# Routing stage of a graph layer with experts: layer-norm sums taken from the quotient, squared deviations on the scalar engine

## The reference

```python
x = x + gnn(xn) + mix(xn)
h = (x - mean(x)) / sqrt(var(x) + 1e-5)
logits = h @ gate_w + gate_b
idx = argmax(softmax(logits));  prb = its probability
pos = cumsum(one_hot(idx)) * one_hot(idx) - 1        # place of the row at its expert
buf[idx, pos] = h                                     # dropped when pos >= C
y = relu(buf @ w1[e] + b1[e]) @ w2[e] + b2[e]
x = x + y[idx, pos] * prb
```

## Time and profile before

| | us |
|---|---|
| time, three runs | median 3505.42 (3503.37 to 3508.54) |
| profiled execution | 3478.89, its span 3477.1 |
| routing stage, from the first instruction to the last scatter's end | 2908.4 to 3008.4 |
| first instruction of `experts` | 3014.1 |
| busy over the span | PE 2543.0, DVE 2333.8, POOL 1813.2, ACT 1147.3 |

### The profile page before, as it was taken

The page is one execution under the profiler, slowest core; times in us unless marked ns, Lnnn a source line. Parts: engine busy times, 40 slices in busy tenths (PEclk is TensorE's granted clock), DMA queues, the critical chain, the costliest instruction groups (busy, mean ns, idle before and its releaser), DMA issues. The chain is left out here.

```text
span 3477.1 us, 46302 instructions
## 1 busy us (share of the span) xinstructions
PE 2543.0 (73%) x11245; PEld 1939.2 (56%) x11245; DVE 2333.8 (67%) x7089; ACT 1147.3 (33%) x4204; POOL 1813.2 (52%) x1892
## 2 busy tenths in 40 slices
PE   8577777777777777794676656566666757599998
PEld 6465555656555556683555544444544536476766
DVE  6788887878787778884555545556666668353535
ACT  5543443434343434341222110122332202334342
POOL 0366666666666666304666666666666663311112
PEclk9789998989888989897787777777787775699999
DMA  6566777777767777314555654643444443412120
GB/s 198 161 189 202 205 206 206 207 203 207 203 202 199 205 205 202 103 57 125 149 156 153 169 161 121 181 112 107 112 113 113 112 115 105 138 49 87 54 90 13
DMA packets 230864, 512.62 MB, mean 147 GB/s; under 512 B 49248, under 2 KB 116043, under 8 KB 230610
## 3 DMA queue, kind: packets, MB, share of 16 engines
q0 software_dynamic: 118128, 361.70, 37.1%
q1 hardware_dynamic: 97958, 134.64, 12.8%
q10 hardware_dynamic: 14524, 13.40, 1.1%
HBM read 463.94 MB, written 49.57 MB: 148 GB/s over the span
## 5 line engine op out<-in xcount | busy, mean ns | idle before, releaser
L1306 POOL DMA_INDIRECT weights<-table,SRC x880 | 840.3, 955 | 599.2 <-issue 234.0
L808 POOL DMA_INDIRECT w_G<-table,SRC x880 | 848.0, 964 | 506.2 <-issue 236.5
L910 PE MATMUL PS<-w_G,w_S 128*128 128x260 f32 x3520 | 936.8, 423 | 120.7 <-DVE ACC L986 100.9
L910 PEld LDWEIGHTS PS<-w_G,w_S 128*128 128x128 f32 x3520 | 715.8, 210 | 256.1 <-issue 127.9
L1485 PE MATMUL PS<-weights 128*128 128x257 f32 x1760 | 592.5, 483 | 56.5 <-issue 28.0
L1680 DVE TENSOR_TENSOR ACC<-ACC,PS 128x257 f32 x464 | 196.3, 423 | 451.8 <-remote 247.1
L1485 PEld LDWEIGHTS PS<-weights 128*128 128x128 f32 x1760 | 396.3, 244 | 143.8 <-issue 64.0
L986 DVE TENSOR_TENSOR ACC<-ACC,PS 128x520 f32 x464 | 320.3, 690 | 201.0 <-remote 120.6
L841 ACT ACTIVATE w_G<-w_G 128x64 f32<-128x64 f32 x1760 | 444.3, 335 | 7.1
L979 DVE TENSOR_TENSOR w_G<-w_G,PS 128x512 f32<-128x512 f32 x660 | 432.3, 682 | 4.7 <-ACT ACC L847 4.2
L1325 ACT ACTIVATE w_PW<-w_Z 128x4 f32<-128x4 f32 x220 | 45.2, 205 | 930.6 <-DVE w_Z L1665 731.2
(11 more groups left out here) (323 smaller groups left out, 3309.6 us busy)
## 6 DMA issues: line engine op xcount, KB each, us to landing
w_DR<-rows SPq DMA_DIRECT2D x146, 384.0 KB
weights<-in_L_ffn_w SPq DMA_DIRECT2D x16, 1024.0 KB, 7.9
w_G<-table,SRC POOLq DMA_INDIRECT x880
weights<-table,SRC POOLq DMA_INDIRECT x880
table<-ACC SPq DMA_DIRECT2D x49, 260.0 KB
xbuf<-XR SPq DMA_DIRECT2D x8, 1040.0 KB
XR<-xbuf SPq DMA_DIRECT2D x7, 1040.0 KB, 5.8
table<-row ACTq DMA_DIRECT2D x49, 129.0 KB, 2.2
```

The costliest lines, as they stand in the source:

```text
L808: pool.indirect_dma_start(G[:, r, b, :], None, table, IndexOn(ap=SRC[:, n * B + b:n * B + b + 1], axis=0)).then_inc(fetched[r], 16)
L910: last = pe.matmul(PS[:, 2 * at + a, 0:W // layer.banks], lhsT, rhs, start=b == slots[0], stop=b == slots[-1])
L1306: pool.indirect_dma_start(G[:, r, b, :], None, table, IndexOn(ap=SRC[:, n * B + b:n * B + b + 1], axis=0)).then_inc(fetched[r], 16)
```

## The change

`quotient` writes the row's sum as well (`accum_out`). `bn_stats` and six of the seven operations of `spread` go; what is left of it, the product of the sum with the gate's column sums, becomes `means(g)` and moves to the head of `choose(g)`. The scalar engine computes the squared deviations: `square(t)` takes `(sum - 256 x)^2` with the sum as its bias and accumulates over the row, two tiles ahead of the copy (`SQUARES = 2`). The root takes that sum with scale and epsilon folded in. `sums` issues plain quotients, no longer one ahead: with AHEAD still 3, the quotients up to b + 2 stand before `choose(g)` and those up to b + 4 before `assign(g)`.

```diff
-AHEAD, LEAD, ROOT = 3, 3, 2
+AHEAD, LEAD, ROOT, SQUARES = 3, 3, 2, 2
             def quotient(t):
-                dve.scalar_tensor_tensor(x1(t), ACC[:, t, 0:D], RD[:, t:t + 1], x1(t), ALU.mult, ALU.add).then_inc(x1_ready, 1)
-
-            def statistics(t):
-                dve.wait_ge(x1_ready, t + 1)
-                return dve.bn_stats(bn[:, t, :], x1(t))
+                dve.scalar_tensor_tensor(x1(t), ACC[:, t, 0:D], RD[:, t:t + 1], x1(t), ALU.mult, ALU.add,
+                                         accum_out=total[:, t:t + 1]).then_inc(x1_ready, 1)
             def sums(a, b):
                 for t in range(a, b):
-                    if t == 0:
-                        quotient(0)
-                    if t + 1 < TILES:
-                        quotient(t + 1)
-                    last = statistics(t)
-                    if t + 1 in AT:
-                        own_.link(last)
-                        spread(AT.index(t + 1) - 1)
-            def spread(g):
+                    quotient(t)
+
+            def means(g):
...
-                own_.link(dve.tensor_tensor(ta[:, s], bn[:, s, 1], bn[:, s, 4], ALU.subtract))
-                own_.link(dve.scalar_tensor_tensor(ta[:, s], ta[:, s], 0.25, ta[:, s], ALU.mult, ALU.mult))
-                own_.link(dve.tensor_tensor(va[:, s], bn[:, s, 2], bn[:, s, 5], ALU.add))
-                own_.link(dve.tensor_scalar(va[:, s], va[:, s], 1.0 / D, EPS, ALU.mult, ALU.add))
-                dve.tensor_tensor(ta[:, s], ta[:, s], va[:, s], ALU.add).then_inc(to_root, 1)
-                own_.link(dve.tensor_tensor(me[:, s], bn[:, s, 1], bn[:, s, 4], ALU.add))
-                own_.link(dve.tensor_tensor(LG[:, s, :], one(me[:, s], 2, EXPERTS), one(gs[:, :], 1, w), ALU.mult))
+                dve.wait_ge(x1_ready, AT[g + 1])
+                own_.link(dve.tensor_tensor(LG[:, s, :], one(total[:, s], 2, EXPERTS), one(gs[:, :], 1, w), ALU.mult))
             def choose(g):
...
+                means(g)
                 dve.wait_ge(rooted, g + 1)
...
+            def square(t):
+                if t < TILES:
+                    act.wait_ge(x1_ready, t + 1)
+                    if t >= 3:
+                        act.wait_ge(squared, t - 2)
+                    act.activation(gone[:, t % 3, :], XR[:, t, D:2 * D], ACT.Square, bias=total[:, t:t + 1], scale=-float(D),
+                                   accum_out=squares[:, t:t + 1]).then_inc(squared, 1)
             def root(g):
-                act.wait_ge(to_root, g + 1)
-                act.activation(ta[:, s], ta[:, s], ACT.Sqrt).then_inc(rooted, 1)
+                act.wait_ge(eps_ready, 1)
+                act.wait_ge(squared, AT[g + 1])
+                act.activation(ta[:, s], squares[:, s], ACT.Sqrt, bias=eps[:, 0:1], scale=float(D) ** -3).then_inc(rooted, 1)
...
+            for t in range(SQUARES):
+                square(t)
             for g in range(len(PARTS)):
                 for t in range(AT[g], AT[g + 1]):
                     copy(t)
...
                     if g > 0 and t == AT[g] + LEAD:
                         weights(g - 1)
+                    square(t + SQUARES)
```

More of the change, by code:

```diff
@@ L2060, in deliver @@
         RD = dev["rstd"]
-        bn = dev["DST"][:, 0:6 * TILES].rearrange("p (t a) -> p t a", a=6)
-        me, va, ta = (sb(n, [P, TILES]) for n in ("me1", "va1", "ta1"))
+        total, squares, ta = (sb(n, [P, TILES]) for n in ("total1", "squares1", "ta1"))
+        gone, eps = sb("gone1", [P, 3, D]), sb("eps1", [P, 1])
         r1, nm = XR[:, :, AT_R], XR[:, :, AT_NM]
@@ L2079, in deliver @@
         x1_ready, own, record = sem("r_x1_ready"), sem("r_own"), sem("r_record")
-        to_root, rooted = sem("g_to_root"), sem("g_rooted")
+        squared, rooted, eps_ready = sem("g_squared"), sem("g_rooted"), sem("g_eps")
         turned, copied, lg_done, gate_sum = sem("g_turned"), sem("g_copied"), sem("lg_done"), sem("g_gate_sum")
@@ L2145, in spread @@
                     dve.wait_ge(gate_sum, 1)
-                    own_.link(dve.tensor_scalar(gs[:, :], PS[:, 6, 0:EXPERTS], 0.5, None, ALU.mult))
-                own_.link(dve.tensor_tensor(ta[:, s], bn[:, s, 1], bn[:, s, 4], ALU.subtract))
-                own_.link(dve.scalar_tensor_tensor(ta[:, s], ta[:, s], 0.25, ta[:, s], ALU.mult, ALU.mult))
-                own_.link(dve.tensor_tensor(va[:, s], bn[:, s, 2], bn[:, s, 5], ALU.add))
-                own_.link(dve.tensor_scalar(va[:, s], va[:, s], 1.0 / D, EPS, ALU.mult, ALU.add))
-                dve.tensor_tensor(ta[:, s], ta[:, s], va[:, s], ALU.add).then_inc(to_root, 1)
-                own_.link(dve.tensor_tensor(me[:, s], bn[:, s, 1], bn[:, s, 4], ALU.add))
-                own_.link(dve.tensor_tensor(LG[:, s, :], one(me[:, s], 2, EXPERTS), one(gs[:, :], 1, w), ALU.mult))
+                    own_.link(dve.tensor_scalar(gs[:, :], PS[:, 6, 0:EXPERTS], 1.0 / D, None, ALU.mult))
+                dve.wait_ge(x1_ready, AT[g + 1])
+                own_.link(dve.tensor_tensor(LG[:, s, :], one(total[:, s], 2, EXPERTS), one(gs[:, :], 1, w), ALU.mult))
             def choose(g):
@@ L2164, in all_ @@
                     return one(row, 1, w)
+                means(g)
                 dve.wait_ge(rooted, g + 1)
                 own_.link(dve.reciprocal(r1[:, s], ta[:, s]))
-                own_.link(dve.scalar_tensor_tensor(nm[:, s], me[:, s], -0.5, r1[:, s], ALU.mult, ALU.mult))
+                own_.link(dve.scalar_tensor_tensor(nm[:, s], total[:, s], -1.0 / D, r1[:, s], ALU.mult, ALU.mult))
                 dve.wait_ge(lg_done, b)
@@ L2199, in _ @@
             own_.link(dve.memset(BASE[:, 0, :], 0.0))
+            dve.memset(eps[:, :], EPS).then_inc(eps_ready, 1)
             done = 0
```

## The result

The changed kernel takes 3520.23 us (median of five, 3516.12 to 3526.47) against 3506.22 (five, 3503.37 to 3512.87): ratio 1.0040, 95% interval 1.0029 to 1.0050. It is slower by 14.0 us; a second set of five gave 1.0037 (1.0023 to 1.0051), 3521.60 against 3508.62. The forecast was 3513.4 with 3500 to 3519: slower was its likeliest direction, and the time lies 1.2 us beyond the range. As differences: +8 was forecast from 3505.4, at most +13.6, and +14.0 came.

The account below looks back on a forecast made before the run. The tensor engine's pace and hand-overs set group 3's `put`: 27 tiles at 1.17 and three changes at 4.6, then 32 scatters, ending at 3010.4. Between +6.4 and +8.9, +8 was taken on 3505.4: 3513.4 us, range 3500 to 3519.

Parts of the forecast that it names:

- The prices: Scalar engine: 0.49 us per accumulating square; vector engine: 0.47 us per quotient with a sum, 75 ns per accumulator read.
- The hand-overs: At each group change in the routing stage the tensor engine loses 4.6 us together, besides 1.17 per tile.
- steps 2 and 4: Group change, tensor engine waiting for quotients: 1.3 us lost behind `choose`, 1.0 behind the counts and `assign`.
- steps 1, 3 and 4: Group change, products waiting for copies: 0.8 us behind root and square, then 0.5 and 0.5 for squares queued before copies.
- Rival C: Group changes cost the tensor engine only 0.8 + 0.5 us each; 3497.5 us; chance 0.10 for anything on this side.
- rival D: Square isn't in the square root's table: a load follows each root, 1.28 us more per change, +4, 3517; chance 0.04.
- Step 1: Start of a group change: behind root, its table load and a square, the tensor engine's product loses 0.8 us, 0.33 before.
- the other price: 1.38 us of draining per table load at the root: loss 2.2 instead of 0.8, sum near 3517; given no chance.
- Rival B: The remote stall misses the stage or falls where GpSimd has a backlog: +2, 3507.4; chance 0.36.
- the stall term: GpSimd ahead of group 4: the same 8.46 us remote stall in both kernels costs 6.9 now, 4.43 before; stage +8.9.

Follow-up runs that it names:

- e5: Changed kernel with all scatters issued behind the last group's put: 3528.48 us, +52.7, ratio 1.0146.
- f4: Changed kernel with a 256-column memset on GpSimd behind each scatter and a wait for it: one profile, not timed, stage end at 127.8 us.
- f2: Changed kernel with AHEAD 4 and all scatters behind the last put: one profile, not timed, last put at 77.6 us.
- f3: Changed kernel without its squares and with all scatters behind the last put: one profile, not timed, last put at 80.2 us.
- e3: Kernel before with its quotients in plain order, statistics and `spread` kept on the vector engine: 3521.26 us, +10.4, ratio 1.0027.
- f1: Kernel before with all scatters behind the last put: one profile, not timed, last put at 76.4 us.
- e1: Changed kernel with AHEAD 4 instead of 3: 3514.26 us, +3.4, ratio 1.0010.
- after_again: Changed kernel run once more, beside the kernel before on the same chip: 3521.60 us, +13.0, ratio 1.0037.
- e4: Changed kernel without the 49 squares, the variance left out and the root taken of a constant: 3515.56 us, +4.7, ratio 1.0012.
- e6: Changed kernel with all output transfers issued behind the last group: 3501.31 us, +25.5 against the kernel before on the same chip, ratio 1.0073.
- e8: Changed kernel with AHEAD 6, square root and reciprocal replaced by logarithm and exponential: 3484.28 us, +8.5 against the kernel before on the same chip, ratio 1.0025.
- f5: Changed kernel with every scatter destination out of bounds, so no rows are scattered: one profile, not timed, stage end at 112.6 us.
- f6: Changed kernel scattering a constant tile instead of `XR`'s rows: one profile, not timed, stage end at 112.9 us.
- b_again: Kernel before run once more, unchanged, for a second profile: 3477.39 us, one time.
- f9: Kernel before with a short 128-column memset, without a wait, behind each scatter of group 3: 3509.86 us, -1.1, ratio 0.9995.
- f7: Changed kernel with AHEAD 6 and, in groups 0 to 2, a 256-column memset and wait behind each scatter: 3507.39 us, -3.6, ratio 0.9985.
- f8: Changed kernel, AHEAD 6, waited-for 256-column memsets behind scatters of groups 0 to 2, unwaited 128-column ones in group 3: 3506.06 us, -4.9, ratio 0.9983.
- e2: Changed kernel with AHEAD 6 instead of 3: 3511.68 us, +0.8, ratio 1.0005.

## Why the prediction missed: its steps one by one

**The prices were about right.** The scalar engine's rows show a square and the copy behind it (timeline of after):

```profile
2937.03 0.49 ACT L2208 ACTIVATE gone<-XR,total 128x256 f32<-128x256 f32 x1
2937.43 0.19 ACT L2208 ACTIVATION_READ_ACCUMULATOR gone<-XR,total 128x1 f32 x1
2937.52 0.36 ACT L2201 ACTIVATE XT<-PS 128x256 f32<-128x256 f32 x1
```

From 2937.03 to 2937.52 is 0.49, the figure that was put together from the earlier trace rows. The quotient with a sum repeats every 0.40 us (3018.72 to 3019.12), below the 0.47 taken and equal to the lower bound (beside group 2's scatters some repeat after 0.46 to 0.47); its read takes 80 ns, 75 were taken from the earlier trace rows.

**The hand-overs were right.** A change was to cost 4.6 us, and the one shown costs 4.9; group 3's `put` was to come 60.1 us into the stage and comes at 60.5 (e5) or 60.7 (f4) where nothing stalls; group 4's 16.3 behind it, and it is 16.7. This is no luck of two errors that cancel, since the single waits agree too. Against e5, f2 takes the tensor engine's waits for quotients, in steps 2 and 4, from 10.6 to 0.7 us, and f3 its waits for copies, in steps 1, 3 and 4, from 4.9 to 0.5. Taking 22 us of vector work out of the stage gained nothing by itself. e3 keeps that work, has the plain order, and loses 10.4 us.

**Rival C (hand-overs hide) fell** on the waits of 0.61 to 1.22 us, **rival D (a load at each square)** on ten loads, none of them at the squares. Step 1's 0.90 us, with a load in it, also answers the other price: the Trainium skill, "ScalarE: Activation LUTs", What ACT_TABLE_LOAD costs, adds a drain of 1.38 us to each, and neither that wait nor the 1283 ns of the load's own row has room for it. At the change shown, the load starts at 2958.51, 0.02 behind the end of a copy, and the root at 2959.81, 0.02 behind the load's; the measurement decides. **Rival B (the stall goes) fell** too, and this is where the sum went wrong.

**The step that failed** is the stall term: "With it in both at the same place, it costs 8.46 - 1.6 = 6.9 now and cost 4.43 before". It treated the stall as one event of a fixed length at a fixed place, taken over from the earlier trace rows. It is neither. It comes with scatters that GpSimd issues closely in a row (e5 without them beside the tiles and f4 with gaps between them have none), and the changed kernel has a second one and a longer first one. From the forecast's +8.9 for the stage to the measured +16.0:

- hand-overs up to group 3: 6.8 instead of 6.4 (53.7 before, 60.5 without stalls), +0.4;
- a stall inside group 3's own tiles, beside group 2's scatters: put 3 at 65.4, not 60.5, +4.9. Forecast: none;
- group 4: GpSimd idle 9.35 instead of 4.43, so 4.9 more where 2.5 was forecast, +2.4. Of the 26.95 us between the two puts, 16.75 are the work (e5) and 10.2 the stalls; before it was 22.5, 13.7 (f1) and 8.8;
- scatters of 0.97 us all along, where some took 1.16 before: -0.6.

The sum is 8.9 + 0.4 + 4.9 + 2.4 - 0.6 = 16.0. Its two terms for the stalls, 7.3 together, make up the 7.1 us that were missing.

**Why group 3 stalled only after the change** is only partly settled. Rows of GpSimd in the kernel before, among group 2's scatters (timeline):

```profile
2946.42 1.14 POOL L2109 DMA_INDIRECT xbuf<-XR,put  x1 [0.30 <-issue]
2947.87 1.14 POOL L2109 DMA_INDIRECT xbuf<-XR,put  x1 [0.30 <-issue]
```

These start 1.45 us apart and take 1.14; five of the group's seven gaps are 1.42 to 1.47 us, and the other two 1.28 and 1.29. Those of after start 1.28 apart and take 0.97 (2970.53, 2971.81). The Trainium skill, "SBUF — State Buffer", Who interferes with whom, has a vector instruction with two inputs in that memory contend with a GpSimd instruction that reads it. The trace agrees only in part: in the kernel before a scatter takes 1.14 beside quotients and statistics and 0.98 beside `spread`'s small operations (2950.76), but in after and in e3 it takes 0.97 beside quotients too. So what stretched the gaps before isn't shown. It would be simple to say that the removed statistics had kept the scatters apart, but e3 speaks against that: it has all its statistics, and group 2's scatters are at 1.28 (timelines of GpSimd and scalar in e3):

```profile
2980.55 0.97 POOL L2109 DMA_INDIRECT xbuf<-XR,put  x1 [0.30 <-issue]
2981.82 0.98 POOL L2109 DMA_INDIRECT xbuf<-XR,put  x1 [0.30 <-issue]
...
2990.79 0.66 ACT L2211 ACTIVATE XT<-PS 128x256 f32<-128x256 f32 x2 [3.90 <-remote]
```

With the plain order it stalls in group 3 like the changed kernel (3.90 us), so the statistics needn't go. The shorter lead isn't needed either: e1 has the old lead back and stalls there too (2.73 us ahead of one copy). What separates the profiles is the pace of group 2's scatters. In all ten in which its seven gaps are 1.27 to 1.28 us (after, after_again, e1 to e4, e6, e8, f5, f6) copies in group 3's tiles are late, the worst of each profile 2.9 to 4.9 us behind its transpose; in the six in which they are wider (before, b_again and f9, five of seven at 1.42 or more; f4, f7 and f8, all at 2.09 or more) none is over 0.5. Near the edge it varies: in f9, which is the kernel before up to there, the copy of the next group's first tile comes 1.7 us behind, in the other two it doesn't. At 1.36, in group 3, stalls stay (f8, f9). This compares kernels that differ in other things too, so it supports the pace as the cause without isolating it.

The length of a dense run may count as well: in those ten, the first late copy (over 0.5 us) belongs to a turn issued 2.8 to 5.9 us behind the group's first scatter, and beside the short groups 0 and 1 the worst copy is 1.9 us behind (e2). No run tests it.

**What stays open:** which path inside the chip is held up by closely issued scatters, so that the tensor engine's completions reach the scalar and vector engines late. Some are let go among the scatters, and none later than 2.4 us behind the end of the group's last one. It isn't the written data (f5), the source (f6) or the output transfers (e6). Also open are whether the pace or GpSimd's wait for its memset helps in f4, what sets the pace of 1.45 in the kernel before, and why f9's stalls go on into group 4's scatters.

## What to carry to other kernels

Work taken from an engine that already runs ahead of the one that bounds buys nothing, while the order that the move brings with it (here one tile less of lead, and a square queued in front of a copy) can be paid at every hand-over: restore the lead first, and look at the result then (e1: 3.4 of 14.0 us are left). A wait in the profile whose releaser makes no sense is a term with a cause, not a constant: before adding it to a sum, repeat the profile and find out what it depends on, by moving or spacing what ran beside it. Small shifts in how densely one engine issues can bring a stall elsewhere that costs more than the edit.

## What the runs showed of the hardware, unexpected

- Beside indirect scatters that GpSimd issues 1.28 us apart, the scalar and vector engines saw results of the tensor engine late: 12.6 us of waits before the copies in a stage of 116 (after), up to 8.35 us ahead of a single copy (f7). With starts 2.10 us apart and a memset and its wait between them (f4), or with the scatters behind the tiles (e5), it was zero.
- Scatters whose rows are all out of bounds cause it as well (9.7 us, f5).
- An accumulating quotient (fp32, 256 columns) costs the vector engine 0.40 us from start to start, with its 80 ns read inside it (after, 3018.72 to 3019.12).
- Spacing is nearly free where GpSimd waits anyway (f7: group 3's first scatter starts 1.1 us behind its `put`, 0.8 in after) and costs its whole length where GpSimd is the bound (f4's stage: 127.8).
- Logarithm and exponential alternated at one table load each (1.283 us), twelve in all (e8).
